# A bias row summed by VectorE instead of fp32 matmuls in a four-layer conditional residual kernel

## The reference, cut to what matters

```python
x = x + L0(x)   # shared gated MLP (1024 wide) and two chosen of 8 skill MLPs, softmax-weighted
x = x + L1(x)   # the argmax expert of 8: silu(x Wup' + bu) * (x Wgate' + bg), times Wdown', + bd
x = x + L2(x)   # x (sum_g y[b, g] weight[g] * mask)' + bias2
x = x + L3(x)   # x Wbase' + b_base + 2 * lora(x, y)
# lora: h = einsum('btc,erc->bter', x, As); einsum('bter,eor,be->bto', h, Bs, y)
```

## Time and profile before

| | before |
|---|---|
| median of 3 runs (range) | 494.03 us (493.86 to 494.21) |
| the profiled execution, its own time | 494.58 us |
| its span, first to last instruction | 493.0 us |
| granted TensorE clock, mean of the core | 0.999 |
| TensorE matmul busy | 488.1 us, 99%, 2284 instructions |
| VectorE busy | 345.9 us, 70%, 568 instructions |
| ScalarE busy | 249.9 us, 51% |
| GpSimd busy | 29.8 us, 6% |
| moved by DMA | 49.71 MB, 115972 packets |

### The profile page before, as it was taken

One profiled execution on the slowest core, in us unless ns is written; L12 is line 12 of the kernel. 1 busy time (PEld: TensorE's weight loads), 2 busy tenths in 40 slices (PEclk: granted clock), 3 DMA queues, 4 the chain that ended last, 5 costly groups with the idle time before them and its releaser, 6 DMA issues.

```text
span 493.0 us, 7453 instructions
## 1 busy us (share of the span) xinstructions
PE 488.1 (99%) x2284; PEld 408.3 (83%) x2284; DVE 345.9 (70%) x568; ACT 249.9 (51%) x386; POOL 29.8 (6%) x52
## 2 busy tenths in 40 slices
PE   8999999999999999999999999999999999999997
PEld 6887888888888888888888888888888888888897
DVE  4868889967536578985743758997664466899566
ACT  4555645645536444654554544555454444456452
POOL 1920300000000200000000020000000002000000
PEclk9999999999999999999999999999999999999999
DMA  7888995267220432129440232404842024320001
GB/s 220 154 171 219 234 207 154 64 165 146 77 64 0 128 109 77 53 87 196 101 128 0 63 108 68 124 14 151 153 127 64 0 64 125 110 64 0 0 2 44
DMA packets 115972, 49.71 MB, mean 101 GB/s; under 512 B 66472, under 2 KB 114736, under 8 KB 115952
## 3 DMA queue, kind: packets, MB, share of 16 engines
q1 hardware_dynamic: 113504, 44.32, 35.5%
q0 software_dynamic: 2448, 5.15, 3.8%
HBM read 47.34 MB, written 2.10 MB: 100 GB/s over the span
## 4 chain that ended last, share of the span: by engine, by line
PE 98%; DMA 1%; SPq 0%; DVE 0%; DVEq 0%; issue 0%
PE bank_a L990 10%; PE bank_a L991 10%; PE bank_a L992 10%; PE bank_b L992 10%; PE bank_b L990 10%; PE bank_b L991 10%; PE out L1008 9%; PE out L1012 9%; PE out L1009 9%; PE tail L990 1%; PE tail L992 1%; PE tail L991 1%; PE tail L1008 1%; PE tail L1012 1%; PE tail L1009 1%; DMA raw<-in_L_cond_shared_up 1%
## 5 line engine op out<-in xcount | busy, mean ns | idle before, releaser
L480 ACT ACTIVATE hid_hi<-hid 128x512 fp32r<-128x512 f32 x108 | 68.3, 632 | 109.2 <-DVE hid L602 64.0
L475 ACT ACTIVATE hid<-bank_a 128x512 f32<-128x512 f32 x96 | 57.3, 597 | 82.3 <-PE bank_a L992 81.8
L609 DVE TENSOR_TENSOR hid_lo<-hid,hid_hi 128x512 fp32r<-128x512 f32 x108 | 74.2, 687 | 14.0 <-ACT hid_hi L480 14.0
L591 DVE TENSOR_TENSOR w_lo<-raw,w_hi 128x768 fp32r<-128x768 f32 x88 | 83.5, 949 | 0.0
L602 DVE SCALAR_TENSOR_TENSOR hid<-bank_b,mine,hid 128x512 f32<-128x512 f32 x64 | 48.0, 750 | 40.1 <-PE bank_b L992 38.8
L467 ACT ACTIVATE w_hi<-raw 128x768 fp32r<-128x768 f32 x88 | 73.7, 838 | 0.0
L990 PE MATMUL bank_a<-x_hi,w_hi 128*128 (+1 forms) x176 | 68.6, 390 | 0.0
L991 PE MATMUL bank_a<-x_lo,w_hi 128*128 (+1 forms) x176 | 68.6, 390 | 0.0
L992 PE MATMUL bank_a<-x_hi,w_lo 128*128 (+1 forms) x176 | 68.5, 389 | 0.0
L990 PE MATMUL bank_b<-x_hi,w_hi 128*128 (+1 forms) x176 | 68.5, 389 | 0.0
L991 PE MATMUL bank_b<-x_lo,w_hi 128*128 (+1 forms) x176 | 68.5, 389 | 0.0
(11 more groups left out here) (242 smaller groups left out, 711.3 us busy)
## 6 DMA issues: line engine op xcount, KB each, us to landing
raw<-in_L_cond_skill_gate SPq DMA_DIRECT2D x32, 256.0 KB, 3.0
raw<-in_L_cond_skill_up SPq DMA_DIRECT2D x32, 256.0 KB, 3.2
raw<-in_L_cond_skill_down SPq DMA_DIRECT2D x64, 128.0 KB, 3.2
raw<-in_L_cond_shared_down SPq DMA_DIRECT2D x26, 128.0 KB, 3.6
raw<-in_L_cond_shared_gate SPq DMA_DIRECT2D x12, 256.0 KB, 3.0
raw<-in_L_cond_shared_up SPq DMA_DIRECT2D x12, 256.0 KB, 3.3
raw_gate<-in_L_cond_W_gate SPq DMA_DIRECT2D x16, 128.0 KB, 3.2
early<-in_L_cond_weight POOLq DMA_DIRECT2D x2, 1024.0 KB, 9.6
```

Source lines behind the costliest of these rows:

```text
L475: nc.scalar.activation(hid[:, n % 2], bank_a[n % 2][:, :], func, **kw).then_inc(act_ready, 1)
L480: nc.scalar.activation(hid_hi[:, n % 2], hid[:, n % 2], ACT.Copy).then_inc(hid_hi_ready, 1)
L591: nc.vector.tensor_tensor(lo, raw[:, raw_slot(i // 2), :, (i % 2) * P:(i % 2 + 1) * P], hi.bitcast(F32), ALU.subtract).then_inc(split_lo, 1)
L609: nc.vector.tensor_tensor(hid_lo[:, n % 2], hid[:, n % 2], hid_hi[:, n % 2].bitcast(F32), ALU.subtract).then_inc(hid_lo_ready, 1)
```

## The change

The three bias matmuls and all that fed them alone (u3_y, bias2_m, bias3_b, bias_row) go. VectorE sums the row with the 256 outputs on partitions (two columns of 128) instead:

- GpSimd loads W_base (base_nat, 256 KB, into the free half of raw_gate1) and Bs (b3_nat, runs of 64 B, into bias_all) once more in natural layout, behind the mask; b_base comes as a column. Then it waits for u3, writes it as 128 elements to a scratch in DRAM and reads it back as a row on all partitions. All of this stands before the L2 weights in its queue.
- `bias_base` (chunk 8): two tensor_tensor_reduce of 128x256 give Wbase bias2, then two additions on 128x2.
- `bias_lora` (chunk 13): Bs times the u3 row, 128x256, and a reduction over r to 128x16.
- `bias_columns` (chunk 23): the weighting by y of four batches, its reduction, and the sum with the base.
- Two scattered DMAs write the columns to the scratch `bias_rows`; the broadcast to bias_all follows, now after the first batch's last chunk.
- a3_lo moves from chunk 8 to chunk 10, ahead of b3_y_lo, and counts in l3_lo; c_product waits for l3_lo at 2 in place of 1, and the tail bank has one use less.
- SyncE's waits before the L1 weights change accordingly: W_gate also for the two base sums, W_down for the base sums and a3_lo, W_up for b3_y_lo as before.

```diff
-PREP_AT = {3: "route", 8: "bias"}
+PREP_AT = {3: "route"}
+L3_HI_AT = 8
+BIAS_BASE_AT = 8
+BIAS_LORA_AT = 13
+BIAS_AT = 23
...
+        base_nat = raw_gate1[:, 1, :].rearrange("p (k d) -> p k d", k=KD)
+        b3_nat = bias_all[:, 0, :].rearrange("p (k e r) -> p k e r", k=KD, e=E)
+        u3_row = bias_all[:, 1, 0:P].rearrange("p (e r) -> p e r", e=E)
...
-            free = ((l3_turn, 2),
-                    (tail_free, PREPS.index("bias") + 1),
-                    (l3_lo, 1))
+            free = (((l3_turn, 2), (base_sums, KD)),
+                    ((l3_turn, 2), (base_sums, KD), (l3_lo, 1)),
+                    ((l3_lo, 2),))
...
+            pool.dma_start(base_nat, t["L3_cond_W_base"].rearrange("(k p) d -> p k d", p=P)).then_inc(bias_nat_in, 16)
+            for k in range(KD):
+                pool.dma_start(b3_nat[:, k], t["L3_cond_Bs"][:, k * P:(k + 1) * P, :].rearrange("e p r -> p e r"))\
+                    .then_inc(bias_nat_in, 16)
+            pool.wait_ge(u3_done, 1)
+            pool.dma_start(u3_dram.rearrange("a p -> p a"), u3[:, :], allow_slow_non_contiguous=True).then_inc(u3_out, 16)
+            pool.wait_ge(u3_out, 16)
+            pool.dma_start(bias_all[:, 1, 0:P], u3_dram.broadcast_to([P, P])).then_inc(u3_in, 16)
             pool.wait_ge(tail_ready, PREPS.index("x") + 1)
             pool.wait_ge(x_turn, B - 1)
...
-            pool.wait_ge(bias_row_ready, 1)
-            pool.dma_start(bias_dram, bias_row[:, :]).then_inc(bias_rows_out, 16)
-            pool.wait_ge(bias_rows_out, 16)
+            pool.wait_ge(bias_cols_ready, 1)
+            for k in range(KD):
+                pool.dma_start(bias_dram[:, k * P:(k + 1) * P].rearrange("b p -> p b"), bias_cols[:, k],
+                               allow_slow_non_contiguous=True).then_inc(bias_rows_out, 16)
+            pool.wait_ge(bias_rows_out, 32)
...
-                chain(nc.vector.tensor_tensor_reduce(out=u3_work, in0=a3, in1=bias2_rows, scale=1.0,
-                                                     scalar=0.0, op0=ALU.mult, op1=ALU.add, accum_out=u3[:, :]))
-                nc.vector.tensor_scalar(u3_y[:, :], y_lora[:, :], u3[:, 0:1], None, ALU.mult)
-                nc.vector.tensor_copy(bias2_m[:, :, :], bias2[:, :].unsqueeze(2).broadcast_to([P, KD, B]))\
-                    .then_inc(l3_turn, 1)
+                nc.vector.tensor_tensor_reduce(out=u3_work, in0=a3, in1=bias2_rows, scale=1.0, scalar=0.0,
+                                               op0=ALU.mult, op1=ALU.add, accum_out=u3[:, :]).then_inc(u3_done, 1)
...
+            def bias_base():
+                dve.wait_ge(rows_moved, 16)
+                dve.wait_ge(bias_nat_in, 48)
+                dve.wait_ge(u3_done, 1)
+                for k in range(KD):
+                    nc.vector.tensor_tensor_reduce(out=u3_work, in0=base_nat[:, k], in1=bias2_rows, scale=1.0, scalar=0.0,
+                                                   op0=ALU.mult, op1=ALU.add, accum_out=base_sum[:, k:k + 1])\
+                        .then_inc(base_sums, 1)
+                    dve.wait_ge(base_sums, k + 1)
+                chain(nc.vector.tensor_tensor(base_b[:, :], base_b[:, :], bias2[:, :], ALU.add))
+                chain(nc.vector.tensor_tensor(base_b[:, :], base_b[:, :], base_sum[:, :], ALU.add))
+            def bias_lora():
+                dve.wait_ge(u3_in, 16)
+                chain(nc.vector.tensor_tensor(b3_u3, b3_nat, u3_row.unsqueeze(1).broadcast_to([P, KD, E, R]), ALU.mult))
+                chain(nc.vector.tensor_reduce(b3_sum, b3_u3, op=ALU.add, axis=AX.X))
+            def bias_columns():
+                y = picks[:, :, 5:PICK].unsqueeze(1).broadcast_to([P, KD, B, E])
+                chain(nc.vector.tensor_tensor(b3_shares, b3_sum.unsqueeze(2).broadcast_to([P, KD, B, E]), y, ALU.mult))
+                chain(nc.vector.tensor_reduce(bias_cols[:, :, :], b3_shares, op=ALU.add, axis=AX.X))
+                nc.vector.scalar_tensor_tensor(bias_cols[:, :, :], bias_cols[:, :, :], LORA_SCALE,
+                                               base_b[:, :].unsqueeze(2).broadcast_to([P, KD, B]), ALU.mult, ALU.add)\
+                    .then_inc(bias_cols_ready, 1)
             def l3_operand_lo():
+                dve.wait_ge(l3_hi, 1)
+                nc.vector.tensor_tensor(a3_lo[:, :], a3, a3_hi[:, :].bitcast(F32), ALU.subtract).then_inc(l3_lo, 1)
                 dve.wait_ge(l3_hi, 2)
                 nc.vector.tensor_tensor(b3_y_lo[:, :], b3_y, b3_y_hi[:, :].bitcast(F32), ALU.subtract).then_inc(l3_lo, 1)
...
                 if first(b):
                     pe.wait_ge(tail_free, len(PREPS))
-                    pe.wait_ge(l3_lo, 1)
+                    pe.wait_ge(l3_lo, 2)
...
-                    pe.wait_ge(l3_turn, 3)
-                    rows = tail[0:B, 0, 0:D]
-                    nc.tensor.matmul(rows, u3_y[:, :], b3_t[:, :], start=True, stop=False)
-                    for k in range(KD):
-                        ins = nc.tensor.matmul(rows, bias2_m[:, k], base_t[:, k], start=False, stop=k == KD - 1)
```

More of the change, by code:

```diff
@@ L165, in build @@
         bias2 = sb("bias2", [P, KD])
-        bias2_m = sb("bias2_m", [P, KD, B])
+        base_b = sb("base_b", [P, KD])
+        bias_cols = sb("bias_cols", [P, KD, B])
         bias2_rows = raw_down1[:, 2, :]
         u3 = sb("u3", [P, 1])
-        u3_y = sb("u3_y", [P, B])
+        base_sum = sb("base_sum", [P, KD])
         u3_work = raw_down1[:, 3, :]
-        bias3_b = sb("bias3_b", [B, D])
-        bias_row = sb("bias_row", [B, D])
         bias_all = sb("bias_all", [P, B, D])
+        base_nat = raw_gate1[:, 1, :].rearrange("p (k d) -> p k d", k=KD)
+        b3_nat = bias_all[:, 0, :].rearrange("p (k e r) -> p k e r", k=KD, e=E)
+        u3_row = bias_all[:, 1, 0:P].rearrange("p (e r) -> p e r", e=E)
+        b3_u3 = bias_all[:, 2, :].rearrange("p (k e r) -> p k e r", k=KD, e=E)
+        b3_sum = bias_all[:, 3, 0:KD * E].rearrange("p (k e) -> p k e", k=KD)
+        b3_shares = bias_all[:, 3, D // 2:D // 2 + KD * B * E].rearrange("p (k b e) -> p k b e", k=KD, b=B)
         out_sb = sb("out_sb", [P, NQ, D])
@@ L227, in build @@
         l3_turn = sem("l3_turn")
-        bias_row_ready = sem("bias_row_ready")
+        bias_cols_ready = sem("bias_cols_ready")
+        base_sums = sem("base_sums")
+        bias_nat_in = sem("bias_nat_in")
+        u3_done = sem("u3_done")
+        u3_out = sem("u3_out")
+        u3_in = sem("u3_in")
         l3_in = sem("l3_in")
@@ L365, in _ @@
             expert_pieces(0, 0, {1: lambda: load_x(2), 2: lambda: load_x(3)})
-            free = ((l3_turn, 2),
-                    (tail_free, PREPS.index("bias") + 1),
-                    (l3_lo, 1))
+            free = (((l3_turn, 2), (base_sums, KD)),
+                    ((l3_turn, 2), (base_sums, KD), (l3_lo, 1)),
+                    ((l3_lo, 2),))
             def load_first_l1(n):
-                sp.wait_ge(*free[n])
+                for done in free[n]:
+                    sp.wait_ge(*done)
                 load_l1(sp.value_load(chosen[0:1, 2:3], min_val=0, max_val=E - 1), *l1_weights[n])
@@ L480, in hidden_hi, with l3_operand_hi @@
                 nc.scalar.activation(hid_hi[:, n % 2], hid[:, n % 2], ACT.Copy).then_inc(hid_hi_ready, 1)
[L482 to L487, removed]
+            def l3_operand_hi():
+                act.wait_ge(l3_in, 48)
+                nc.scalar.activation(a3_hi[:, :], a3, ACT.Copy).then_inc(l3_hi, 1)
+                act.wait_ge(l3_f, 1)
+                nc.scalar.activation(b3_y_hi[:, :], b3_y, ACT.Copy).then_inc(l3_hi, 1)
             def later_x_hi(b):
@@ L547, in batch @@
                         hidden_hi(b, n)
-                    if first(b) and i in PREP_AT:
-                        prep_hi(PREP_AT[i])
+                    if first(b) and i == L3_HI_AT:
+                        l3_operand_hi()
                     if first(b) and i in X_HI_AT:
@@ L787, in prep @@
                 dve.wait_ge(tail_ready, PREPS.index(what) + 1)
[L788 to L800, removed]
+                sums = tail[:, 0, 0:B * PICK]
+                nc.vector.tensor_copy(chosen[0:1, :].rearrange("p (b n) -> p b n", n=3),
+                                      sums[0:1, :].rearrange("p (b n) -> p b n", n=PICK)[:, :, 2:5])\
+                    .then_inc(chosen_ready, 1)
+                nc.vector.tensor_copy(picks[:, :, :].rearrange("p b n -> p (b n)"), sums).then_inc(tail_free, 1)
             def x_turn_blocks(b):
@@ L913, in batch @@
                         l3_operand_lo()
+                    if first(b) and i == BIAS_BASE_AT:
+                        bias_base()
+                    if first(b) and i == BIAS_LORA_AT:
+                        bias_lora()
+                    if first(b) and i == BIAS_AT:
+                        bias_columns()
                     if with_tail:
```

10 lines of the change are left out of this document (5 added, 5 removed).

## The result

The changed kernel takes 498.14 us (median of 5, 497.86 to 501.11) against 494.03 (median of 5, 493.64 to 494.21): ratio 1.0105, 95% interval 1.0091 to 1.0118. (The quotient of the two medians is 1.0083; the ratios in this text are not exactly such quotients.) The kernel is slower by 1%, where 0.3% faster was forecast. All executions compared are in the fast state; the one that was not, 995.84 us in run e3, is left out of its ratio. The profiled execution took 498.14 us with a span of 496.6.

A forecast was written before the change was run, and what follows sets the result against it. TensorE, busy 488.1 of 493.0 us, was taken as the bound. Profiled 494.58 - 1.62 (bias products) + 0.30 (wait at c_product) = 493.26; the median lies 0.55 lower: 492.7 us, 8-in-10 range 492.3 to 493.8.

The forecast's parts named there:

- The gross gain, 1.62 us: TensorE, chunk 8: without the bias products it falls from 5.70 to 4.08 us, everything later may start 1.62 us sooner.
- bias_base, 1.32 us under 0.65 us of cover: VectorE, chunk 8: the base sums take 1.32 us and fit before hid of chunk 9 with 0.65 us to spare.
- c_product, 0.30 us: TensorE at c_product: a new wait of 0.30 us for b3_y_lo, now behind a3_lo on VectorE; bounds 0 to 1.2.
- rival B: No new wait at c_product: VectorE is 0.3 us faster than counted, all 1.62 us stay, 492.4 us; chance 0.10.
- Later VectorE work: bias_lora at chunk 13 and bias_columns at chunk 23 cost nothing; uncovered they would be 0.9 and 0.8 us.
- u3's round trip, "cover 3.6 us, cost nothing": GpSimd's queue ahead of the L2 weights: write landing taken as 8.6 us, cover 3.6 us, cost nothing.
- Net delay of SyncE's issues by the added loads, 0 to 1.5 us: base_nat and b3_nat from about 28 us delay SyncE's issues 0 to 1.5 us; W_down's wait takes up 1.6.
- W_down's wait for a3_lo: SyncE's queue: W_down starts 1.6 us later; 0 to 1.6 us lost, 0 to 1.5 given back, taken as zero.
- The limit of 78.5: W_up must have landed by 78.5 us for the down product of chunk 16, 0.8 us later than before.
- Rival D: A load lands over 0.8 us later than before: 0.5 to 1.1 us lost, 493.2 to 493.8 us; chance 0.12.
- Rival E: Slower: u3's write takes so long that the L2 weights are issued late, 495.1 us and up; chance 0.07.
- The rule that the prediction left out of its sum: VectorE's two-port mode locks GpSimd out of writing descriptors; two issues hold its queue 5 us longer, some 0.5 us above forecast.

The follow-up runs named there:

- e3: Kernel before with the changed kernel's two added loads (W_base and Bs) on GpSimd's queue, read by nothing: 493.97 us, ratio 1.0006.
- e6: Kernel before without the three fp32 bias matmuls and nothing in their place: 493.05 us, ratio 0.9979.
- e1: Changed kernel without the write of u3 to the scratch, the broadcast row read from the L2 bias instead: 494.28 us, ratio 1.0021.
- e5: Changed kernel with u3 and bias columns transposed in 32x32 blocks first, so both writes go in 128 B runs: 492.87 us, ratio 0.9988.
- e8: Changed kernel with the bias row's feeds issued behind chunk 15's transposes, sums in chunks 22 and 23, a3_lo in chunk 8, 4-byte writes: 492.50 us, ratio 0.9973.
- e10: Changed kernel with writes in 128 B runs and a3_lo back in chunk 8, added loads left in place: 492.31 us, ratio 0.9977.
- e11: Repeat of e7 on the same chip as e9 and e10: 492.28 us, ratio 0.9976.
- e4: Kernel before with u3's round trip through the scratch added ahead of the L2 weights, its row read by nothing: 497.00 us, ratio 1.0070.
- e2: Changed kernel with Bs loaded in 256 runs of 512 B instead of 2048 short ones: 498.50 us, ratio 1.0107.
- e9: Changed kernel unaltered, measured again on the same chip as e10 and e11: 498.77 us, ratio 1.0109.
- e7: Changed kernel with the bias row's feeds issued behind chunk 15's transposes, sums in chunks 22 and 23, a3_lo in chunk 8, 128 B writes: 492.36 us, ratio 0.9982.

## Why the prediction was wrong

Point by point:

- **The gross gain, 1.62 us**: right. Chunk 8 fell to 4.08 us, and e6 gives 0.25 to 1.8 us of time, 1.0 by its ratio and 0.8 between the medians.
- **bias_base, 1.32 us under 0.65 us of cover**: right. It took 1.28 and left 0.77.
- **c_product, 0.30 us**: right in mechanism, and near in size where the loads are in time: chunk 11 takes 0.37 us more than before in e1 and 0.60 in e5 (0.8 of wait in the changed kernel, where VectorE was late from a split). But a3_lo in front of b3_y_lo is only part of it: with a3_lo in chunk 8, 0.24 to 0.36 remain (e6 to e8, e10, e11), so rival B, no loss at all there, was not to be had by that either.
- **Later VectorE work**: right, no wait in its chunks; the reduction over r took 0.42 us, for 0.46 taken.
- **u3's round trip, "cover 3.6 us, cost nothing"**: this is the step that failed. Its own terms nearly held: the write landed 9.2 us after its issue (8.6 taken), GpSimd was free at 49.8 (50.3), the L2 weights left at 53.23 (53.9). But only GpSimd's queue was counted. What the write does to SyncE's loads was no term of the sum and no rival; its price alone is 3.4 us on the kernel before (e4), and removing it or giving it runs of 128 B takes 4 to 6 us from the changed kernel (e1, e5). In the changed kernel it held the third skill piece, so that TensorE lost 4.94 us at chunk 11.
- **Net delay of SyncE's issues by the added loads, 0 to 1.5 us**: mis-sized. By the raw starts it was 2.1 (e3, 39.08 for 36.98) to 2.9 (39.87); against e4, which has no added loads and starts as early as these two, 2.7 and 3.5 (36.37). The bytes were added up against the share in which the engines stood idle over 27 us; but SyncE issues in order and was held in the busiest part of it: before the change the DMA share was 0.95 from 27 to 37 and 0.86 from 37 to 54.
- **W_down's wait for a3_lo, "0 to 1.6 lost, 0 to 1.5 given back"**: mis-sized. With the loads' delay on top it made W_up 3.6 us late for VectorE (e5), 1.8 us of chunk 17. The limit of 78.5 was rightly worked out and then passed: W_up came at 79.58 in a timeline that is 0.77 ahead, so 1.85 us past it, and 1.81 were lost.
- **The cover of the third skill piece** was in no row: ScalarE's split of chunk 12 was the first to need a late load, not the two transfers that VectorE waited for before. A queue in order makes every later load late, and the one to check is the next to be used.
- **Rival D** is what is left without the small write: a load that lands late, 1.05 us at chunk 17 in e1 and 1.8 in e5, for 0.5 to 1.1 taken. **Rival E** had the sign, not the place: the L2 weights weren't issued late. The rule that the prediction left out of its sum, GpSimd locked out beside VectorE, showed nothing here: the two added issues took 0.57 and 0.56 us.

The Trainium skill ("DMA: Bandwidth & Descriptors", section "Issuing engines are not separate DMA queues") says that the DMAs of all issuing engines run on the same 16 engines; the trace agrees (SyncE's issue of 4.82 us ended with GpSimd's write; in e2 and e9 the stretched issues ended 0.9 and 1.5 us behind it). Its section "Specifications" puts a read-modify-write under everything below 512 B. By size alone that doesn't divide these runs: 128 B, which is below it too, landed in 3.3 us and left 177 GB/s while it ran, for 185 before (e5), and the 64 B runs of the loads into SBUF, with W_base, left 171 from 28 to 38, for 199 (e3); only with the 4-byte runs into DRAM did all queues together fall below 70.

What stays open: why they hold the engines. The windows from 45 to 50 show a DMA share of 0.34 to 0.55 at 19 to 66 GB/s (changed kernel, e2, e4, e9), the one from 117 to 122 a share of 0.89 at 23, so the engines were partly busy and partly idle, and no run here separates the engine's own work from the wait for DRAM. The size of the runs (4 and 128 B) and their number (128 and 4) changed together, and so did the number of partitions read, so it is not shown which of them counts. Nor was a row written in 4-byte runs by another queue tried.

## What to carry to other kernels

Before hanging a small transfer into a schedule, ask what it does to the transfers of other queues in its 10 us, not only how long its own queue waits: 512 bytes written in 128 runs of 4 cost more here than 6 fp32 matmul records saved. A column on 128 partitions that must go through DRAM is transposed in 32x32 blocks first, and goes in a stretch in which no load is soon needed. And a load queue in order is checked at its next reader, for every load behind the delayed one.

## What the runs showed of the hardware

- 128 runs of 4 bytes from SBUF to DRAM: 8.1 to 9.2 us from the start of the issue to landing, during which all queues together move 19 to 66 GB/s in the window from 45 to 50 (e9, e4, the changed kernel, e2), 186 to 264 in the runs without it there; 4 runs of 128 B: 2.7 to 5.0 us (e10, e5, e11, e7), 177 GB/s while it ran in e5. Over the whole of the first write in 4-byte runs it was 91 (changed kernel) and 104 (e4), for 212 before.
- 1024 runs of 4 bytes: 11.0 us (113.53 to 124.57) to 12.4 (e8), down to 23 GB/s, not eight times the 128 runs'. 32 runs of 128 B took 4.3 us (110.22 to 114.51, e5).
- Reads in 4-byte runs into SBUF (the y rows, 8 DMAs of 64 elements) landed in 2.7 us (median, from the profile before).
- An idle stretch of TensorE of 2.67 us was followed by 3 us at the lower clock in one execution (e9); one of 3.43 us in another was not.
